# Windowed attention and top-1 MoE on one core: batch 0 prepared in halves, the other norms inside the attention, results of two tiles at once

## What is computed

```python
def _L0_attn_ref(x, W_qkv, b_qkv, W_out, b_out):      # NH, WINDOW = 16, 32;  HD = 128 // NH = 8
    qkv = x @ W_qkv + b_qkv
    q, k, v = ...                                      # 16 heads of 8 features
    scores = einsum('bnid,bnjd->bnij', q, k) / sqrt(HD)
    diff = idx[:, None] - idx[None, :]
    scores = where((diff < 0) | (diff >= WINDOW), -inf, scores)
    out = einsum('bnij,bnjd->bnid', softmax(scores), v)
    return out @ W_out + b_out

def _L0_ffn_ref(x, ...):                               # 7 routed experts of 512 hidden features, and no expert at index 7
    probs = softmax(x @ w_router)                      # 8 choices
    out = 2.0 * (largest prob) * expert_of_that_choice(x)
    shared = (x @ ws_up * silu(x @ ws_gate)) @ ws_down
    return out + shared

x = x + _L0_attn_ref(_layernorm(x), ...)
x = x + _L0_ffn_ref(_layernorm(x), ...)
```

## Time and profile before

| | |
|---|---|
| time, median of 3 runs | 367.31 us (366.27 to 370.47) |
| time of the profiled execution | 367.33 us |
| its span, first to last instruction | 365.6 us |
| granted TensorE clock, mean | 0.973 of 2.4 GHz |
| PE busy | 330.0 us, 90% of the span |
| DVE busy | 225.6 us, 62% |
| ACT busy | 176.4 us, 48% |
| POOL busy | 174.9 us, 48% |

### The profile page before, as it was taken

The page is one execution under the profiler, slowest core; times in us unless marked ns, Lnnn a source line. Parts: engine busy times, 40 slices in busy tenths (PEclk is TensorE's granted clock), DMA queues, the critical chain, the costliest instruction groups (busy, mean ns, idle before and its releaser), DMA issues. The chain is left out here.

```text
span 365.6 us, 12604 instructions
## 1 busy us (share of the span) xinstructions
PE 330.0 (90%) x5014; PEld 260.7 (71%) x5014; DVE 225.6 (62%) x539; ACT 176.4 (48%) x313; POOL 174.9 (48%) x256
## 2 busy tenths in 40 slices
PE   8788999899999898997967999979999999999980
PEld 8545665565656555885855888868898999989970
DVE  4966997788988978779442333333555455554540
ACT  1646666567666575663221222214455554555530
POOL 6652455464557566692674444462333333333331
PEclk9989999999999999999889999998999999999996
DMA  8965333334433321000121111213222232222200
GB/s 207 357 219 149 90 109 98 97 105 129 133 101 100 102 44 32 2 2 0 37 86 56 67 61 60 88 43 81 77 66 65 69 73 71 67 67 69 74 5 0
DMA packets 40426, 30.66 MB, mean 84 GB/s; under 512 B 5792, under 2 KB 36772, under 8 KB 40370
## 3 DMA queue, kind: packets, MB, share of 16 engines
q1 hardware_dynamic: 36800, 23.17, 23.0%
q0 software_dynamic: 2880, 6.43, 5.0%
q10 hardware_dynamic: 690, 0.26, 0.4%
HBM read 13.72 MB, written 11.95 MB: 70 GB/s over the span
## 5 line engine op out<-in xcount | busy, mean ns | idle before, releaser
L599 POOL DMA_INDIRECT out<-y,tok_u x38 | 37.4, 984 | 72.8 <-DVE y L1199 72.8
L1214 DVE SCALAR_TENSOR_TENSOR Pr<-psS,xs,PT 128x256 f32<-128x256 f32 x76 | 33.3, 480 | 47.6 <-PE psS L1549 47.3
L881 DVE TENSOR_REDUCE row_max<-psS 128x16 fp32r<-128x1024 f32 x32 | 39.1, 1224 | 16.3 <-PE psS L1274 16.1
L1025 DVE TENSOR_TENSOR hT<-psS,PT 128x512 f32<-128x512 f32 x32 | 22.1, 690 | 41.4 <-PE psO L1436 17.1
L768 ACT ACTIVATE PT<-psS 128x512 f32<-128x512 f32 x32 | 19.2, 599 | 58.0 <-PE psS L1424 44.6
L1565 PEld LDWEIGHTS psB<-down_sb,Pr 128*128 128x128 f32 x304 | 40.2, 193 | 4.3 <-issue 1.0
L917 DVE STREAM_TRANSPOSE PT<-Pr 128x1024 f32<-128x1024 f32 x32 | 39.6, 1236 | 2.4 <-ACT Pr L671 2.2
L1565 PE MATMUL psB<-down_sb,Pr 128*128 x304 | 40.3, 276 | 0.8 <-ACT Pr L805 0.8
L428 POOL TENSOR_TENSOR rows<-rows,proj 128x128 f32<-128x128 f32 x31 | 14.2, 458 | 54.9 <-ACT proj L677 52.3
L1303 PEld LDWEIGHTS psO<-VD,PT 128*32 128x32 f32 x2048 | 22.3, 109 | 21.7 <-issue 21.1
L1274 PE MATMUL psS<-Kx,Qx 64*32 64x256 f32 x1024 | 35.1, 384 | 0.8 <-issue 0.8
(11 more groups left out here) (202 smaller groups left out, 730.8 us busy)
## 6 DMA issues: line engine op xcount, KB each, us to landing
sorted_rows<-pad_row SPq DMA_DIRECT2D x19, 264.0 KB
VD<-V SPq DMA_DIRECT2D x120, 36.0 KB, 2.4
xs<-sorted_rows SPq DMA_DIRECT2D x38, 66.0 KB, 2.0
base<-sorted_rows SPq DMA_DIRECT2D x38, 64.0 KB, 1.8
rows<-in_L_attn_x SPq DMA_DIRECT2D x8, 256.0 KB, 5.8
gate_sb<-in_L_ffn_w_gate SPq DMA_DIRECT2D x1, 1792.0 KB, 10.3
up_sb<-in_L_ffn_w_up SPq DMA_DIRECT2D x1, 1792.0 KB, 14.7
down_sb<-in_L_ffn_w_down SPq DMA_DIRECT2D x7, 256.0 KB, 3.4
```

Of the source, the lines that this page charges most:

```text
L599: pool.indirect_dma_start(out=out_list, out_offset=bass.IndirectOffsetOnAxis(tok_u[:, r : r + 1], 0), in_=y[:, r, :], in_offset=None, boun ...
L881: nc.vector.tensor_reduce(row_max[:, k % 2, :], s, AX.X, ALU.max).then_inc(max_done, 1)
L1214: nc.vector.scalar_tensor_tensor(out=hs[:, r % 2, h], in0=psS[:, r % 2, h], scalar=xs[:, q, GATE : GATE + 1], in1=sg[:, r % 2, h], op0=ALU ...
```

## The change

- Batch 0 is prepared in two halves of two tiles. The statistics are aggregated by one VectorE instruction per tile, POOL raises the variance to the power -1/2 for two tiles at a time, and VectorE scales the tiles. TensorE forms the values of the lower half first, then its queries and keys, then the upper half. VectorE writes the keys of the lower half (`first_k_ready`), ScalarE all else.
- The first half of `VD` is zeroed by VectorE, the second by ScalarE, none by POOL. Slot 0 waits for `first_v_ready`, the values of two tiles.
- In batch 0 TensorE turns x of batch 1 after the weighing of tile 0 and forms the values of batch 1 in step 2 and not in step 1; ScalarE writes the keys of batch 1 after the exponentials of tile 2.
- The norms of batches 1 to 7 move: VectorE takes the statistics of batches 1 and 2 in the prologue and those of batches 3 to 7 inside the attention (two tiles in odd steps); POOL forms the factors and scales (`input_ln`).
- Division, transpose, projection, copy and residual work on two tiles at once (a unit); the last two tiles are units of their own. `psO`'s two banks alternate by unit, each with the values of two tiles.
- SP: x of batches 0 to 3 ahead of slot 0; x of batches 4 to 7, the shared weights, the router, and the gate and up weights in three DMAs each stand behind slots 0 to 7, two DMAs a slot (one in slot 0), the down weights behind slots 7 to 10, and two pre-fills behind each of slots 11 to 14, the last eleven behind slot 15.
- POOL does splits in pairs, 16 of the 32 pieces inside the attention, 16 after it (12 before). Constants are made later.
- 64 idle products at the start in place of 128, none later.

The core of the diff:

```diff
-    WARM = 128
-    FILL = 10
+    WARM = 64
...
+    UNITS = NT // 2 + 1
+
+    def unit_of(b, k):
+        g = b * TPB + k
+        return g // 2 + (g == NT - 1)
+
+    def tiles_of(u):
+        return 2 if u < UNITS - 2 else 1
+
+    def first_tile(u):
+        return NT - 1 if u == UNITS - 1 else 2 * u
...
-            for b in range(B):
+            def load_x(b):
...
+            for b in range(4):
+                load_x(b)
...
+                if n == 0 and half == 0:
+                    sp.wait_ge(first_v_ready, 1)
+                    sp.wait_ge(VD_zero, 1)
+                else:
+                    sp.wait_ge(v_ready, n + 1)
+                    sp.wait_ge(VD_zero_late, 1)
...
-            def load_or_pad():
-                e = next(downs, None)
-                if e is not None:
-                    load_down(e)
-                    return
-                piece = next(pads, None)
-                if piece is not None:
-                    sp.wait_ge(pad_ready, 1)
-                    write_pads(piece)
...
                     spread_values(n, half)
-                    load_or_pad()
-                    load_or_pad()
+                    if n == 0 and half == 0:
+                        load_x(4)
+                    elif n < 2:
+                        load_x(4 + 2 * n + half)
+                        load_shared((None, 1, 0, 2)[2 * n + half])
+                    elif n == 2 and half == 0:
+                        load_router()
+                        load_gates(0)
+                    elif n == 2:
+                        load_gates(1)
+                        load_gates(2)
+                    elif n == 3 and half == 0:
+                        load_ups(0)
+                        load_ups(1)
+                    elif n == 3:
+                        load_ups(2)
+                        load_down(0)
+                    elif 2 * n + half < 2 * 4 + 3:
+                        e = 2 * (2 * n + half - 8) + 1
+                        load_down(e)
+                        load_down(e + 1)
+                    else:
+                        sp.wait_ge(pad_ready, 1)
+                        first = 2 * (2 * n + half - 11)
+                        for piece in range(first, MT // PADS if n == B - 1 and half == 1 else first + 2):
+                            write_pads(piece)
...
+            for lo in range(0, TPB, 2):
+                t = slice(lo, lo + 2)
+                pool.wait_ge(first_aggregated, lo + 2)
+                then_first(pool.tensor_scalar(ln_ve[:, t], row_mv[:, t, 1], 1.0, EPS, ALU.mult, ALU.add))
+                pool.tensor_tensor(
+                    rstd[:, t], ln_ve[:, t], power[:, 0:1].to_broadcast([P, 2]), ALU.pow
+                ).then_inc(first_rstd, 1)
...
+            def residual(u):
+                pool.wait_ge(proj_ready, u + 1)
+                g, n = first_tile(u), tiles_of(u)
                 pool.wait_ge(xb_done, g // TPB + 1)
-                xk = x_all[:, g, :]
-                pool.tensor_tensor(xk, xk, proj[:, g % 2, :], ALU.add).then_inc(res_done, 1)
+                xk = x_all[:, g : g + n, :]
+                pool.tensor_tensor(
...
+            def input_ln(b):
+                t = slice(b * TPB, (b + 1) * TPB)
+                moments(b * TPB, (b + 1) * TPB, first=True)
+                deviations(b * TPB, (b + 1) * TPB)
+                then(pool.tensor_tensor(ln_b[:, t], mean[:, t], rstd[:, t], ALU.mult))
+                normalise(b)
...
+            for u in range(EARLY // 2):
+                b, half = divmod(u, 2)
+                residual(u)
+                if half == 0 and b + 3 < B:
+                    input_ln(b + 3)
+                if u >= 2:
+                    for low in range(2):
+                        split(u - 2, low)
+                if half == 1 and b + 2 < B:
                     add_bias(b + 2)
...
-            for n in range(EARLY, NT):
-                split(n // 2, n % 2 == 1)
+            for n in range(SPLITS, 2 * E):
+                for low in range(2):
+                    split(n, low)
...
+            act.wait_ge(zeros_ready, 1)
+            nc.scalar.activation(scratch[:, 0:1], Kx[:, 0, 0, 0:1], ACT.Exp)
+            nc.scalar.copy(
+                VD[:, 2:, :, :, :, :].rearrange("p k c j h v -> p (k c j h v)"),
+                Kx[:, 0, 0, 0:1].to_broadcast([P, TPB // 2 * 2 * NJ * NH * VW]),
+            ).then_inc(VD_zero_late, 1)
...
+            act.wait_ge(v_ones_ready, 1)
+            act.wait_ge(first_v, 1)
+            evict_first_values(0, lower, first_v_ready)
             act.wait_ge(bk_of_ready, 1)
-            evict_q(0, 0, first=True)
-            evict_k(0, 0)
-            act.wait_ge(v_ones_ready, 1)
-            evict_v(0, 0, first=True)
...
+                if k % 2 == 0 and b + k > 0:
+                    evict_proj(unit_of(b, k) - 1)
...
                 if edge is True:
                     evict_xnT(1)
                     evict_q(1, 1, first=True)
-                    evict_k(1, 1)
                 elif edge != "last":
                     evict_k(b + 1, 1 - odd, heads=(2, 3))
                 else:
                     turned_batch(2)
                 step(b, 1, odd, first=edge)
-                if edge != "last":
-                    evict_v(b + 1, 1 - odd, first=edge is True)
+                if edge is True:
+                    evict_k(1, 1)
+                elif edge != "last":
+                    evict_v(b + 1, 1 - odd)
                 else:
                     turned_batch(3)
...
+            nc.vector.memset(VD[:, 0:2, :, :, :, :], 0.0).then_inc(VD_zero, 1)
...
+            def normalise_first(lo):
+                dve.wait_ge(first_aggregated, lo + 2)
+                dve.wait_ge(first_rstd, lo // 2 + 1)
+                for k in range(lo, lo + 2):
+                    last = nc.vector.tensor_scalar(
+                        xn[:, k, :], x_all[:, k, :], row_mv[:, k, 0:1], rstd[:, k : k + 1], ALU.subtract, ALU.mult
+                    )
+                last.then_inc(first_norm if lo == 0 else norm_done, 1)
+
...
+            for h in range(HPG):
+                last = nc.vector.tensor_scalar(
+                    Kx[:, 0, h, BLK : BLK + T // 2], psS[:, 1, 0 : T // 2], head_of[:, h : h + 1], bk_of[:, h : h + 1],
+                    ALU.mult, ALU.add,
+                )
+            last.then_inc(first_k_ready, 1)
+            input_stats(2, 0, TPB)
...
+                u = unit_of(b, k)
                 turn_probs(b, k, first=first)
-                if k > 0:
-                    output(b, k - 1, first=first)
-                elif not first:
-                    output(b - 1, TPB - 1)
-                if k > 1:
-                    moments_after(b, k - 2)
-                elif not first:
-                    moments_after(b - 1, k + TPB - 2)
+                if u > 0 and (k % 2 == 0 or tiles_of(u) == 1):
+                    output(u - 1)
                 if k + 2 < TPB:
                     find_max(b, k + 2, first=first)
                 elif not last:
                     find_max(b + 1, k + 2 - TPB)
+                if k % 2 == 1 and u > 0:
+                    moments_after((b * TPB + k) // 2 - 1)
+                if k == 1 and b + 3 < B:
+                    input_stats(b + 3, 0 if b == 0 else 2, TPB)
...
+            turn_first(0, psA, first_turned)
             pe.wait_ge(bv_wide_ready, 1)
             pe.wait_ge(wout_in, 16)
             pe.wait_ge(bout_in, 16)
             mm(psO[:, 0, 0:D], bv_wide[:, :], wout_sb[:, :], start=True, stop=False)
             mm(psO[:, 0, 0:D], ones[0:1, 0:P], bout_sb[0:1, :], start=False, stop=True).then_inc(bias_mm, 1)
...
+            values_first(0, first_v)
+            mm(psO[:, 1, lower], wqkv_sb[:, 0:D], xnT[:, lower], start=True, stop=True).then_inc(first_q, 1)
+            mm(psS[:, 1, lower], wqkv_sb[:, D : 2 * D], xnT[:, lower], start=True, stop=True).then_inc(first_k, 1)
+            pe.wait_ge(xnT_ready, 1)
+            pe.wait_ge(bias_ready, 1)
+            mm(psO[:, 0, upper], wqkv_sb[:, 0:D], xnT[:, upper], start=True, stop=True).then_inc(q_done, 1)
+            mm(psB[:, lower], wqkv_sb[:, D : 2 * D], xnT[:, upper], start=True, stop=True).then_inc(k_done, 1)
+            pe.wait_ge(first_v_ready, 1)
+            values_first(1, v_done)
             pe.wait_ge(filled, after["masks"])
...
+                u = unit_of(b, k)
+                if u > 0 and b * TPB + k == first_tile(u):
+                    project(u - 1)
                 if k == 0 and edge == "first":
+                    turn_x(1)
                     queries(1)
                     keys(1)
                 if k == 0 and edge not in ("first", "next", "last"):
                     turn_x(b + 2)
-                if k == 1 and edge != "last":
+                if k == 1 and edge not in ("first", "last"):
                     values(b + 1)
-                    if edge == "first":
-                        turn_x(2)
-                if k == 2 and edge not in ("next", "last"):
```

(5 more changed lines are left out.)

457 lines of the change are left out of this document (241 added, 216 removed).

## The result

The kernel of the change takes 369.15 us (median of 20 runs, 365.47 to 372.28), the kernel before beside it 368.38 us (20 runs), so the medians differ by 0.2%. The ratio is 1.0079, with the interval [1.0042, 1.0115]; it leaves out the slow executions of each kernel, those over 1.5% above its fastest, and is therefore not the ratio of the medians. Two later measurements gave 1.0048 [1.0000, 1.0095] and 1.0041 [0.9996, 1.0086]. The kernel before measured against itself gave 0.9934 (e9), so a loss of 0.4 to 0.8% can't be told from none. What is measured is no gain: all three ratios are above 1, where the sum of 366.0 for 367.3 us would be 0.9965.

The account below looks back on a forecast made before the run. SP's DMA issues were taken to pace the attention at 7.77 us a pair, above TensorE's 7.24. The terms summed as 367.33 - 5.0 + 0.5 + 1.9 + 1.3 = 366.0 us, range 361.5 to 372.

Parts of the forecast that it names:

- start of slot 2: Attention: values of batch 1 ready at 31.0 instead of 36.0 us, so slot 2 starts 5.0 us sooner.
- slot 2 to slot 13 (loads): SP's slots: loads of x and weights replace pads and down weights, adding 0.5 us in all.
- slot 13 to slot 15 (pads): End of attention: slots 13 and 14 gain two pads each, 15.2 us instead of 13.3, a loss of 1.9.
- Prologue: Batch 0 in halves: `first_v_ready` at 10.5 us (bounds 9.5 and 12.5), first weighing at 18.5 against 28.14.
- SP paces the attention at 7.77 a pair: Attention: SP issues DMAs all the time, 7.77 us a pair, while TensorE could do 7.24.
- Rival 1: Attention: SP is not the bound, TensorE's 5.0 us lead is kept and pads cost nothing; about 363 us, chance 0.25.
- Splits: After the attention: four more POOL pieces hold VectorE's routing chain by 0 to 4 us, taken as 1.3.
- Norms on POOL: Attention: POOL's 5 us of norms a batch are hidden with under 1 us to spare.
- results of two tiles: Attention: TensorE waits 0.55 us before `project`, a pair takes about 7.7, hidden behind SP's 7.77.
- Rival 2: Attention: a unit's output comes late and the even step waits for VectorE; 371 us at 8.25 a pair, chance 0.15.
- Rival 3: Slots 4 to 7: seven large loads hold SP ahead of spreads; 369 to 372 us, chance 0.12.
- Rival 4: Prologue: batch 0 is not sooner, slot 2 starts at 35, the rest is lost; 370 us, chance 0.06.

Follow-up runs that it names:

- e9: The kernel before with no edit, measured against itself: 368.33 us against 368.30, ratio 0.9934.
- e10: The kernel before with its 12 late split pieces moved into POOL's waits between scatters: 362.38 us against 368.3, ratio 0.9843.
- e5: The kernel of the change with no edit, second trace, on a faster chip: 358.27 us against 357.71 for before, ratio 1.0048.
- e15: The kernel of the change with no edit, third trace: 369.93 us against 370.6 for before, ratio 1.0041.
- e3: The kernel of the change with its 16 late split pieces moved into POOL's waits between scatters: 364.9 us against 369.9 for before, ratio 0.9890.
- e1: The kernel before with down weights and all pads issued behind the last slot, 8 DMAs a slot instead of 10: 364.03 us against 369.9, ratio 0.9849.
- e2: The kernel of the change with bulk loads moved ahead of slot 0, behind slot 1 and behind slot 15: 366.85 us against 369.9 for before, ratio 0.9903.
- e6: The kernel of the change with VectorE's statistics ahead of the row maximum in odd steps: 358.08 us against 357.71 for before, ratio 1.0076.
- e13: The kernel of the change with 12 late split pieces, the other four inside the attention: 371.09 us against 370.6 for before, ratio 1.0000.
- e14: The kernel before with 16 late split pieces beside the routing in place of 12: 373.14 us, ratio 1.0121.
- e4: The kernel of the change with the values of batch 1 projected one step sooner: 368.11 us against 369.9 for before, ratio 0.9956.
- e7: The kernel of the change with the two-tile results undone, each tile by itself: 359.38 us against 357.71 for before, ratio 1.0067.
- e11: The kernel of the change with bulk loads out of the slots and statistics ahead of the row maximum: 362.06 us against 368.3 for before, ratio 0.9855.
- e8: The change with loads out of slots, batch 1 values sooner, statistics first, late pieces between scatters: 356.33 us against 357.71 for before, ratio 1.0015.

## Why the prediction was wrong, point by point

The forecast was 366.0 us, 1.3 below before, and the ratio went the other way. The step that failed is the line "slot 15 and the end of the attention come 5.0 - 0.5 - 1.9 = 2.6 us sooner", with the 1.3 for the pieces behind it. The mechanism held: SyncE paces, pads cost, pieces hold VectorE. The sizes did not. The means below are of three traces with before's attention (before, e9, e10) and four with the change's (after, e5, e15, e3), in us; the row of the pieces is without e3 and e10, which move them.

| term | forecast | before | after | measured |
|---|---|---|---|---|
| start of slot 2 | -5.0 | 35.5 | 32.1 | -3.4 |
| slot 2 to slot 13 (loads) | +0.5 | 85.3 | 87.1 | +1.8 |
| slot 13 to slot 15 (pads) | +1.9 | 14.0 | 16.0 | +2.0 |
| slot 15 to the last division | 0 | 14.1 | 12.7 | -1.4 |
| last division to positions (pieces) | +1.3 | 24.55 | 26.77 | +2.2 |
| sum | -1.3 | | | +1.2 |

Slot 15 starts 0.4 us later, not 2.6 sooner; the attention ends 1.0 us sooner, and the pieces take twice that. The sum of +1.2 us is 0.3%, between the 0.2% of the medians and the 0.4 to 0.8% of the ratios. The traces of one program differ by up to 3 us in the attention, so only the pieces' term is sure to a tenth.

**Prologue: right to 1 us.** `first_v_ready` forecast at 10.5; slot 0 started at 10.83. First weighing 18.5 forecast, 19.36 measured. Slot 2 at 31.0 forecast, 32.04 measured, a gain of 4.0 for 5.0 against the trace shown and 3.4 in the means.

**"SP paces the attention at 7.77 a pair": right in kind, the margin and the cost of a slot wrong.** In before SyncE was the limit, as e1 shows, by 0.25 us a slot; "all the time" was nearly right, with pauses of 2.9 and 4.9 us in 105 in before and e9. In after it still is: it pauses for only 2.1 to 5.4 of 105 us, and with two DMAs a slot gone the slots come 0.5 us closer (e2). What the forecast called hidden, TensorE's longer pair, was there (7.53 to 7.72 in e2, 7.7 forecast) and was hidden, which is why e6 won nothing. But the margin is so thin that what delays TensorE reaches SyncE: in the first trace it stood 4.2 us between slots 7 and 8 beside TensorE's stop. Slots 2 to 15 take 3.8 us more than in before, 2.4 forecast: 2.2 are SyncE's own issues, with four more of them, and 1.5 are its pauses. Rival 1 ("SP is not the bound") is refuted by e1 and e2.

**Last row maximum to last division: 7.50 us in before, 8.60 to 8.98 in after.** Before starts the weighing of (7, 2) without a wait for a DMA, 8.8 to 9.2 us behind slot 15, so a slot 15 that comes a little late costs nothing. In after TensorE is there first and waits for slot 15's DMAs, 1.67 us in e5 and 1.44 in e15 (the 1.46 that the view of after puts down to VectorE is at the same place), and weighs 7.4 to 7.6 us behind it. Timeline of PE of e5:
```profile
144.93 0.76 PE L1410 MATMUL psO<-VD,PT 128*32 128x36 f32 x64 [1.67 <-DMA VD<-V]
```
From this weighing to the last division it takes 5.07 us in before and 5.17 in after. So the 1.1 to 1.5 us lost after the last row maximum are SyncE's slots again. And of the 3.8 us that the slots lose 1.4 did not reach the end, because before had that much slack there.

**Splits: mechanism right, size wrong.** 1.3 was forecast with bounds 0 and 4; it is 2.2, in e13 and e14 alone and to 0.05 us alike. I took a third of four pieces' 4 us because a third of the chain reads PSUM. What counts is which operations fall under the pieces: three of the smallest, with nothing to hide behind, at 0.9, 0.35 and 1.0 us each. The rule of the Trainium skill cited in the forecast ("SBUF — State Buffer", section "SBUF: two separate sides"), that the port pair is held for a whole instruction, agrees: the addition of 0.16 us and the scan of 0.17, both with two inputs from SBUF, end with the instruction of GpSimd that they met. The operation of 0.52 has one such input. The forecast's 4 us, with every piece holding VectorE for its whole length, were 1.8 too many, its 1.3 were 0.9 too few.

**Norms on POOL, results of two tiles.** Hidden, as forecast: TensorE never waited for POOL's scaled rows. Its wait before the projection is 0.3 to 0.4 us, 0.55 forecast.

**Rival 2** (the unit's output comes late) described what the pair does, with a pair of 7.53 to 7.72 instead of 8.25. **Rival 3** (large loads hold SP) had the right suspects and the wrong victim. Gate and up loads issue in 1.10 and 1.43 us a pair, so SyncE is hardly held, and the 2.31 of the earlier trace rows is no cost of a large load as such. TensorE's stops stand beside them: at 68.5 in after, and at 67.9, 69.6, 72.5 and 70.3 in e4, e6, e7 and e13, for 2.1 to 3.3 us; behind the loads' new place in e2 and e11. e3 and e5 have the same loads and no stop on issue over 1.2 us. So the loads go with most of the stops; what ends a stop is told below. **Rival 4** (batch 0 not sooner) is out with slot 0 at 10.83.

## What to carry to other kernels

When the next limit comes out within 2% of the one that paces, as 7.7 under 7.77 here, the sum may go by the pacer, but relief of the other alone is worth nothing (e6), and a stop of either costs both: give such a stage a wider range than the sum's own terms. Ask of each queue how long it pauses; a queue that pauses for 2 to 5 of 105 us is the limit, whatever the busy shares say. Count the slack at the end of the stage as well, in before and in after. Work for GpSimd put beside a chain of tiny VectorE operations costs up to 1 us for each operation that it meets; ask which operations of the chain it meets, not which share of it. And a shortened stage must be followed to the next queue: in e8 11.6 us were won ahead of the scatter, and TensorE then waited 8.09 us for rows.
